# Weight preparation moved from VectorE to GpSimd, and new orders before and after the loop of a decoder layer

## What is computed

```python
x = layernorm(x + mixer(x))        # Mamba-2: W_in, conv of 4 taps, decay, gate, RMS norm, W_out
x = layernorm(x + xattn(ctx, x))   # 8 heads of 64; keys and values of [norm(ctx), norm(x)]
x = layernorm(x + ffn(x))          # 3 cycles: out += coupling * twist(out)

# mixer, the end
y = y * silu(z)
y = y * rsqrt(mean(y * y) + 1e-5) * norm_w
return y @ W_out.T
# ffn
gf = global_net(mean(x))                       # 3 layers, gelu
for _ in range(3):
    tf = coupling_net(out)                     # 4 layers, gelu
    out = out + (0.1 + r * (0.7 * gf + 0.3 * tf - 0.5) * 2) * twist(out)
```

## Time and profile before

| | us |
|---|---|
| median of 3 runs | 3686.03 (3682.52 to 3687.17) |
| profiled execution: its time | 3687.81 |
| profiled execution: span | 3685.6 |
| TensorE busy | 3613.6 (98%) |
| VectorE busy | 3246.4 (88%) |
| ScalarE busy | 3072.9 (83%) |
| GpSimd busy | 1788.0 (49%) |

### The profile page before, as it was taken

One profiled execution on the slowest core, in us unless ns is written; L12 is line 12 of the kernel. 1 busy time (PEld: TensorE's weight loads), 2 busy tenths in 40 slices (PEclk: granted clock), 3 DMA queues, 4 the chain that ended last, 5 costly groups with the idle time before them and its releaser, 6 DMA issues.

```text
span 3685.6 us, 79670 instructions
## 1 busy us (share of the span) xinstructions
PE 3613.6 (98%) x26752; PEld 3085.0 (84%) x26752; DVE 3246.4 (88%) x7970; ACT 3072.9 (83%) x7559; POOL 1788.0 (49%) x3084
## 2 busy tenths in 40 slices
PE   5999999999999999999999999999999999999997
PEld 4888888888888888888888888888888888888885
DVE  7888988988988989889889889889898898898884
ACT  5788888888888888888888888888888888888884
POOL 4355454454554554554544545545545545445442
PEclk8999999999999999999999999999999999999998
DMA  3212212112122122122121121221221221211210
GB/s 100 59 37 67 59 42 67 52 49 67 39 63 64 37 67 64 37 67 58 43 67 53 48 67 39 63 65 37 67 64 37 67 60 42 67 55 46 67 34 21
DMA packets 312358, 203.28 MB, mean 55 GB/s; under 512 B 55056, under 2 KB 310928, under 8 KB 311952
## 3 DMA queue, kind: packets, MB, share of 16 engines
q1 hardware_dynamic: 311952, 198.20, 18.7%
HBM read 180.17 MB, written 17.96 MB: 54 GB/s over the span
## 4 chain that ended last, share of the span: by engine, by line
PE 93%; DVE 3%; ACT 1%; issue 1%; SPq 1%; DMA 1%; POOL 1%; POOLq 0%; DVEq 0%; ACTq 0%
PE psum L263 35%; PE psum L455 10%; PE psum L471 9%; PE psum L443 8%; PE psum L350 6%; PE psum L482 6%; PE psum L518 5%; PE psum L338 5%; PE psum L524 2%; PE psum L533 2%; PE psum L322 1%; PE psum L495 1%; PE psum L383 1%; PE psum L361 1%; PE psum L545 1%
## 5 line engine op out<-in xcount | busy, mean ns | idle before, releaser
L1015 ACT ACTIVATE prob<-psum,nmax 128x376 f32<-128x376 f32 x1024 | 588.7, 582 | 36.0 <-DVE nmax L1741 35.0
L2471 POOL TENSOR_TENSOR Lm<-Lm,G 128x384 f32<-128x384 f32 x512 | 497.3, 1011 | 81.8 <-DVE out_sb L1869 68.8
L1741 DVE TENSOR_REDUCE nmax<-psum 128x2 f32<-128x752 f32 x512 | 472.8, 934 | 44.2 <-PE psum L443 39.4
L455 PE MATMUL psum<-ident,prob 128*128 128x128 f32 (+1 forms) x3072 | 486.4, 278 | 3.1 <-DVE probT L1764 1.7
L455 PEld LDWEIGHTS psum<-ident,prob 128*128 128x128 f32 (+1 forms) x3072 | 354.8, 141 | 87.0 <-issue 46.5
L1493 DVE SCALAR_TENSOR_TENSOR u<-psum,par,u 128x255 f32<-128x255 f32 (+5 forms) x960 | 408.2, 467 | 12.0 <-ACT u L914 1.5
L2458 POOL TENSOR_SCALAR_AFFINE_SELECT Lm<-Lm 128x256 f32<-128x256 f32 x512 | 193.0, 416 | 375.7 <-DMA Lm<-cum_row 375.5
L2526 POOL TENSOR_TENSOR h_a<-h_a,cpl 128x512 f32<-128x512 f32 x64 | 83.0, 1297 | 594.0 <-DVE h_pre L1852 594.0
L471 PE MATMUL psum<-probT,V 128*64 128x256 f32 (+1 forms) x3072 | 360.5, 383 | 0.4 <-ACT probT L1025 0.4
L263 PE MATMUL psum<-x_hi,w_in_hi 128*128 128x256 f32 (+1 forms) x1152 | 344.8, 299 | 13.0 <-DVE w_in_lo L1897 7.6
L263 PE MATMUL psum<-x_hi,w_in_lo 128*128 128x256 f32 (+1 forms) x1152 | 325.4, 282 | 0.0
(11 more groups left out here) (227 smaller groups left out, 11668.6 us busy)
## 6 DMA issues: line engine op xcount, KB each, us to landing
Lm<-cum_row SPq DMA_DIRECT2D x64, 1024.0 KB, 5.2
Lm<-cum_row SPq DMA_DIRECT2D x64, 512.0 KB, 6.6
invT<-inv_row SPq DMA_DIRECT2D x256, 128.0 KB, 3.0
xT_sb<-in_xT SPq DMA_DIRECT2D x64, 256.0 KB, 2.7
x_sb<-in_x SPq DMA_DIRECT2D x64, 256.0 KB, 5.8
result<-out_sb SPq DMA_DIRECT2D x64, 256.0 KB, 2.4
inv_row<-inv_t SPq DMA_DIRECT2D x512, 1.0 KB
ctx_sb<-in_ctx SPq DMA_DIRECT2D x64, 120.0 KB, 6.4
```

The costliest lines, as they stand in the source:

```text
L455: t = tr(banks[b][0:m, j * P:(j + 1) * P], prob[:, r, j0:j0 + m], ident[:, :])
L1015: act(prob[:, r, :], b[:, 0:NK], ACT.Exp, bias=nmax[:, n:n + 1], accum_out=psum_row[:, n:n + 1]).then_inc(a_exp, 1)
L1741: e.tensor_reduce(nmax[:, 2 * n:2 * n + 2], psum[:, b:b + 2, 0:NK], AX.X, ALU.max, negate=True).then_inc(d_max, 1)
L2471: t = tt(Lm[:, h, :], Lm[:, h, :], G[:, :], ALU.mult)
```

## The change

- `w_out_sb`'s scaling and the two subtractions for wkv_lo leave VectorE's `weights` and go, with the same shapes, to GpSimd's `weights`, which becomes `weights(s, n)`. GpSimd runs its old part first (n = 2), then w_out (n = 0), then wkv (n = 1), all ahead of `masked(0, 0)`. They count on a new semaphore, `set_wp`, which `out_proj` (1) and `q_pair`, `k_tile`, `v_tile` (2, beside `set_w` 4) wait for.
- What is left of VectorE's preparation, `weights(0, 3)`, goes from ahead of `cum_dt(0)` to behind `x_dt(0, 1)` and ahead of `gate_silu(0, 0)`. The silu and rounding of B and C and the sums come ahead of most conv taps.
- ScalarE's start has `weights(0, 3)` (wq and wkv high halves) behind `softplus(0)` and `conv(0, 1)`.
- SP has `spread_cum(1)` right behind `load_xT(1)`, and `load_x(1)` behind `load_xT(2)`.
- The end part of all five programs has a new order. The loops are as before, and TensorE's start too.

```diff
 # TensorE
             def out_proj(s):
-                pe.wait_ge(set_w, 4)
+                pe.wait_ge(set_wp, 1)
             def q_pair(s, j):            # k_tile and v_tile alike
-                pe.wait_ge(set_w, 5)
+                pe.wait_ge(set_w, 4)
+                pe.wait_ge(set_wp, 2)
...
             v_tile(last, 2)
             layer(last - 1, 0, 1)
-            turn(last, 6)
-            glob(last - 1, 1)
+            glob(last - 1, 0)
             turn(last, 7)
             layer(last - 1, 0, 2)
+            glob(last - 1, 1)
+            scores(last, 3, 1)
+            turn(last, 8)
             glob(last - 1, 2)
-            turn(last, 8)
-            scores(last, 3, 1)
+            layer(last - 1, 0, 3)
             turn(last, 9)
+            turn(last, 10)
             twisted(last - 1)
-            layer(last - 1, 0, 3)
-            turn(last, 10)
+            turn(last, 11)
             values(last, 0)
-            turn(last, 11)
             layer(last - 1, 1, 1)
             turn(last, 12)
             turn(last, 13)
             layer(last - 1, 1, 2)
             turn(last, 14)
+            layer(last - 1, 1, 3)
             turn(last, 15)
-            layer(last - 1, 1, 3)
+            layer(last - 1, 2, 1)
             values(last, 1)
-            layer(last - 1, 2, 1)
+            layer(last - 1, 2, 2)
+            layer(last - 1, 2, 3)
             w_o(last, 0)
             w_o(last, 1)
-            layer(last - 1, 2, 2)
-            layer(last - 1, 2, 3)
             x2_turn(last)
-            glob(last, 0)
             layer(last, 0, 0)
             layer(last, 0, 1)
+            glob(last, 0)
+            layer(last, 0, 2)
             glob(last, 1)
-            layer(last, 0, 2)
             glob(last, 2)
             layer(last, 0, 3)
             twisted(last)
 # ScalarE, start
+            weights(0, 0)
             x_high(0)
-            weights(0, 0)
             weights(0, 1)
             bcdt(0)
             weights(0, 2)
             conv(0, 0)
-            weights(0, 3)
+            bcdt_th(0)
             softplus(0)
             conv(0, 1)
-            bcdt_th(0)
+            weights(0, 3)
             conv_th(0, 0)
 # VectorE
-                elif n == 3:
-                    ve.wait_ge(w_rest_in, 16 * 13)
-                    for k in range(CT):
-                        t = ts(w_out_sb[:, k, :], w_out_sb[:, k, :], prm("norm_w", k), None, ALU.mult)
-                    t.then_inc(set_w, 1)
...
-                    for k in range(KT):
-                        t = tt(wkv_lo[:, k, :], wkv_raw[:, k, :], wkv_hi[:, k, :].bitcast(F32), ALU.subtract)
-                    t.then_inc(set_w, 1)
...
             bcdt_tap(0, 0)
-            bcdt_tap(0, 1)
             weights(0, 2)
             dt_add(0)
             softplus(0)
-            conv_tap(0, 1, 0)
+            bcdt_tap(0, 1)
             bcdt_tap(0, 2)
-            conv_tap(0, 1, 1)
-            conv_tap(0, 0, 0)
-            conv_tap(0, 1, 2)
-            weights(0, 3)
-            weights(0, 4)
+            bc_silu(0)
+            bc_high(0)
             cum_dt(0)
             cum_da(0)
             cum_scan(0)
...
             x_dt(0, 0)
             x_dt(0, 1)
+            context_stats(0)
+            weights(0, 3)
             gate_silu(0, 0)
 # GpSimd
-            def weights(s):
+            def weights(s, n):
 
                 po.wait_ge(w_rest_in, 16 * 13)
+                if n == 1:
+                    po.wait_ge(set_hi, 4)
+                    for k in range(KT):
+                        t = tt(wkv_lo[:, k, :], wkv_raw[:, k, :], wkv_hi[:, k, :].bitcast(F32), ALU.subtract)
+                    t.then_inc(set_wp, 1)
+                    return
+                if n == 0:
+                    po.wait_ge(par_in_ok, 16)
+                    for k in range(CT):
+                        t = ts(w_out_sb[:, k, :], w_out_sb[:, k, :], prm("norm_w", k), None, ALU.mult)
+                    t.then_inc(set_wp, 1)
+                    return
...
-            weights(0)
+            weights(0, 2)
+            weights(0, 0)
+            weights(0, 1)
             masked(0, 0)
 # SP
             spread_cum(0)
             load_xT(1)
+            spread_cum(1)
+            load_ctx(1)
+            load_xT(2)
             load_x(1)
-            load_ctx(1)
-            spread_cum(1)
-            load_xT(2)
```

More of the change, by code:

```diff
@@ L697, in _ @@
             turn(last - 2, 4)
-            turn(last - 2, 5)
             mean_square(last - 1)
@@ L701, in _ @@
             layer(last - 3, 0, 0)
-            turn(last - 2, 6)
+            turn(last - 2, 5)
             v_tile(last - 2, 2)
@@ L705, in _ @@
             layer(last - 3, 0, 1)
-            turn(last - 2, 7)
-            turn(last - 2, 8)
+            turn(last - 2, 6)
             glob(last - 3, 0)
@@ L711, in _ @@
             scores(last - 2, 3, 1)
+            turn(last - 2, 7)
+            turn(last - 2, 8)
             glob(last - 3, 2)
@@ L752, in _ @@
             y_pair(last, 1)
+            q_pair(last - 1, 1)
+            turn(last - 1, 2)
             y_pair(last, 2)
+            y_pair(last, 3)
             scores(last - 1, 2, 0)
+            v_tile(last - 1, 1)
+            k_tile(last - 1, 3)
             scores(last - 1, 2, 1)
-            y_pair(last, 3)
-            turn(last - 1, 2)
-            k_tile(last - 1, 3)
-            v_tile(last - 1, 1)
+            turn(last - 1, 3)
             x2_turn(last - 2)
-            turn(last - 1, 3)
+            turn(last - 1, 4)
             scores(last - 1, 3, 0)
-            turn(last - 1, 4)
             turn(last - 1, 5)
@@ L804, in _ @@
             scores(last, 1, 0)
+            layer(last - 2, 2, 3)
             turn(last, 1)
@@ L808, in _ @@
             q_pair(last, 1)
-            layer(last - 2, 2, 3)
+            scores(last, 1, 1)
             turn(last, 2)
-            scores(last, 1, 1)
             scores(last, 2, 0)
+            k_tile(last, 3)
             v_tile(last, 1)
-            k_tile(last, 3)
+            scores(last, 2, 1)
             x2_turn(last - 1)
-            scores(last, 2, 1)
             turn(last, 3)
             turn(last, 4)
-            glob(last - 1, 0)
             scores(last, 3, 0)
             turn(last, 5)
+            turn(last, 6)
             layer(last - 1, 0, 0)
@@ L1242, in _ @@
             layer(last - 4, 2, 2)
+            decay(last - 1, 0)
+            values_out(last - 3, 1)
             exp(last - 2, 0)
-            values_out(last - 3, 1)
+            layer(last - 4, 2, 3)
             exp(last - 2, 1)
-            layer(last - 4, 2, 3)
-            decay(last - 1, 0)
+            v_out(last - 2, 0)
             decay(last - 1, 1)
-            v_out(last - 2, 0)
             decay(last - 1, 2)
             cb_out(last - 1)
-            exp(last - 2, 2)
             decay(last - 1, 3)
@@ L1294, in _ @@
             glob(last - 3, 2)
+            turn_out(last - 2, 7)
             exp(last - 2, 13)
@@ L1297, in _ @@
             layer(last - 3, 0, 3)
+            exp(last - 2, 14)
             turn_out(last - 2, 9)
-            exp(last - 2, 14)
             x1_out(last - 1)
@@ L1313, in _ @@
             turn_out(last - 2, 11)
+            layer(last - 3, 2, 0)
             k_out(last - 1, 2)
-            layer(last - 3, 2, 0)
             turn_out(last - 2, 13)
@@ L1388, in _ @@
             turn_out(last - 1, 15)
-            layer(last - 2, 2, 2)
             exp(last, 0)
@@ L1392, in _ @@
             values_out(last - 1, 1)
-            exp(last, 2)
+            layer(last - 2, 2, 2)
             v_out(last, 0)
             turn_out(last, 1)
+            layer(last - 2, 2, 3)
+            exp(last, 2)
             exp(last, 3)
@@ L1400, in _ @@
             exp(last, 6)
+            k_out(last, 3)
             exp(last, 7)
+            exp(last, 8)
             v_out(last, 1)
-            layer(last - 2, 2, 3)
-            exp(last, 8)
-            k_out(last, 3)
+            exp(last, 9)
             x2_out(last - 1)
-            exp(last, 9)
             turn_out(last, 3)
@@ L1410, in _ @@
             exp(last, 11)
+            turn_out(last, 5)
             layer(last - 1, 0, 0)
-            glob(last - 1, 0)
-            turn_out(last, 5)
             keep_a(last - 1)
@@ L1416, in _ @@
             layer(last - 1, 0, 1)
-            glob(last - 1, 1)
+            glob(last - 1, 0)
             turn_out(last, 7)
             layer(last - 1, 0, 2)
+            glob(last - 1, 1)
             exp(last, 12)
             glob(last - 1, 2)
+            layer(last - 1, 0, 3)
+            turn_out(last, 9)
             exp(last, 13)
             exp(last, 14)
-            turn_out(last, 9)
-            layer(last - 1, 0, 3)
             keep_b(last - 1)
@@ L1433, in _ @@
             layer(last - 1, 1, 2)
-            turn_out(last, 15)
             layer(last - 1, 1, 3)
             layer(last - 1, 2, 0)
+            turn_out(last, 15)
+            layer(last - 1, 2, 1)
```

(6 more changed lines are left out.)

476 lines of the change are left out of this document (238 added, 238 removed).

## The result

The changed kernel takes 3693.74 us (median of 22 runs, 3690.14 to 3698.75), the kernel before, timed with it, 3687.52 (22 runs, 3681.56 to 3692.5). The ratio is 1.0018, 95% interval 1.0011 to 1.0024: slower by 6.2 us. The forecast of 3687.0 was too low, and the range ended 0.24 us short.

The account below looks back on a forecast made before the run. TensorE was taken as busy throughout the middle, with idle time only at both ends. Start −4.5 and end +5.5 gave +1.0 on the profiled execution, 3688.8; the median, 1.8 lower, was forecast at 3687.0 us, range 3680.5 to 3693.5.

Parts of the forecast that it names:

- Step (1): Start, VectorE: without the moved weight work the scan ends near 17.4, ten microseconds earlier; the broadcast lands at 26.1.
- (2): Start, GpSimd: moved scalings (3.6 us) and subtractions (5.0) stand ahead of `masked(0)`, which starts at 31.1 instead of 36.20.
- Step (3): Start, VectorE: second `x_dt(0)` ends near 30.6, or 35.6 if GpSimd's subtractions hold VectorE twice; before 40.22.
- step (4): Start, VectorE: six leftover weight instructions, 2.3 us, fall beside `times_g(0)`; 6 more if each waits for GpSimd.
- Step (5): Start's sum: `times_g(0)` ends near 42, not 46.92; steps behind unchanged, lower clock +0.5 to +1.5; gain 4.5 us.
- rival B: Start: GpSimd's long instructions hold VectorE's silus, then the leftovers; gain 1 or none, about 3692 us; chance 0.20.
- step (6): End, TensorE: `values(last,1)` behind `layer(last-1,2,1)` leaves a gap empty, so `w_o(last,0)` starts 4.0 us later.
- step (7): End, ScalarE: `twisted(last-1)` moved behind `layer(last-1,0,3)` and two turns delays h1 of the third cycle; +0.8 us.
- Step (8): Last sequence: `glob(last)` leaves a wait and stands ahead of `layer(last,0,3)`; +0.7 us, between 0.3 and 1.2.
- A: The end does not lose: −4.5 to −6 at the start, little at the end, 3681.5 us; chance 0.20.
- C: Both ends gain, −7 at the start and −1 at the end: 3678 us; chance 0.08.
- D: The new order causes a stall in the busy stretch: +8, 3694 us; chance 0.05.

Follow-up runs that it names:

- e8: e1 with the low half of wkv made by VectorE again, ahead of the first `x_silu`: 3679.00 us, ratio to the kernel before 0.9972 to 0.9989.
- e7: The change with 25 throwaway matmuls that fit TensorE's wait ahead of `layer(last-1,2,1)`, order unchanged: 3689.77 us, ratio to the kernel before 1.0001 to 1.0019.
- e10: e1 with the change's order of `glob(last)` on TensorE and ScalarE alone: 3685.49 us, ratio to the kernel before 0.9985 to 1.0003.
- e15: The change with old places for values, inverses' round trip, `glob(last)`, GpSimd's `att(last)` and VectorE's x2 norm: 3686.52 us, ratio to before 0.9999.
- e3: The change with `values(last,1)` back ahead of `layer(last-1,2,1)` and `w_o(last)` ahead of `layer(last-1,2,2)`: 3694.85 us, ratio to the kernel before 1.0008 to 1.0025.
- e1: The change's start with the five old endings of the kernel before: 3683.59 us, ratio to the kernel before 0.9979 to 0.9997.
- e6: e1 with throwaway matmuls in TensorE's waits of the last sequence: 3674.06 us, ratio to the kernel before 0.9959 to 0.9981.
- e11: e8's start with e6's throwaway matmuls in the last sequence, old endings: 3673.52 us, ratio to the kernel before 0.9948 to 0.9973.
- e12: e11 with throwaway matmuls in TensorE's waits of the first sequence too: 3685.10 us, ratio to the kernel before 0.9983 to 1.0001.
- e2: The start of the kernel before with the change's five new endings: 3698.05 us, ratio to the kernel before 1.0016 to 1.0039.

## Why the prediction was wrong

**The start, right in the number, in part by luck.** Step (1) and (2): scalings 0.91 (0.90 taken), subtractions 2.5, `masked(0)` at 31.52 (31.1). Step (3) went the other of its two ways: `x_dt(0,1)` ended at 35.98, its held case (35.6). Of the 5.4 above the free case (30.6) the two silus' hold is 3.9; the rest is VectorE's wait for ScalarE, 2.03 where 0.6 was taken. In step (4) the leftovers took 2.2 and were not held; it was GpSimd that waited, three of its `times_g` taking 4.06 beside VectorE's 1.21 of `wq_lo`, and three later ones 2.92. By the Trainium skill (SBUF — State Buffer, Who interferes with whom) a VectorE instruction with two SBUF inputs takes part in the lock with GpSimd; 5.25 us for two `x_silu` beside 5.09 on GpSimd agrees, and so does GpSimd's 5.60 in e8.

Step (5) has `out_proj(0)` at 48.6, measured 48.94, a gain of 4.2 (4.5). But its way there was another: it had `times_g(0)` end near 42, and it ended at 44.43, only 2.5 earlier than before. "The steps behind are the same" did not hold either: before, they began with a wait for `load_xT(1)` behind `in_z(0)`, and this wait is gone. `times_g` was 2.4 us later than forecast, and the steps behind it took 4.5 in place of 6.2; the two nearly cancel. What the gain follows is the start of `in_z(0)`, 4.25 earlier, and thus VectorE's chain to `x_dt(0)`. So the first half of rival B, the held silus, stands on the way that counts. Its second half did not come, and so `gate_silu(0,0)` started at 39.03, where B had it end at 44.6.

**Wrong, step (6), the size of the end.** It forecast 3 us of empty wait (3.08), `w_o(last)` later by 4.0, with step (7) 4.8. Measured from `w_o(last-1)`: 7.72. The parts: h1 later by 0.74, step (7)'s 0.8; the new order at the full clock 4.09, step (6)'s 4.0 (from `layer(last-1,2,1)` to `w_o(last)` it takes 5.30 in e7, 1.21 before); and 2.89 for the clock, which e7 gives back. This last term was not in the sum: it took `layer(last-1,2,1)` and the values at 1.13 and 2.82, their durations from the earlier trace rows, where no long wait stood ahead of them. The prediction allowed for the lower clock level at the start (0.5 to 1.5) and forgot it at the end, where it opened a gap itself. The mechanism was right, a term was missing.

**Step (8)** was 0.7; e10 measures 0.89. **Step (7)**: the 0.74 are there one cycle earlier already (the start of `layer(last-1,1,1)` in e15, 0.66 later than before).

**Missed altogether:** the inverses' round trip (VectorE's transposition, SP's `spread_inv`) and GpSimd's `factors` ahead of the norm. In the change they cost nothing, since the late values cover the one and the late `w_o` the other; so the sum did not need them. But it said nothing of them, and the attempt to mend the values' place alone (e3, on the median no gain) ran into them.

**The middle,** taken at 0 between 0 and 2. From the repeated part to `out_proj(last)` the seven kernels with old endings (before, e1, e6, e8, e10, e11, e12) take 335.56 to 336.45 us, mean 336.1, the ten with new ones 336.34 to 337.57, mean 336.8; and from there to `w_o(last-1)` 34.2 against 34.5. That is 1.0 us of loss; which of the moves makes it, no run shows. The repeated part itself spreads from 3026.99 to 3031.51 over the profiles with no regard to the ends (means 3029.3 with the old endings, 3029.0 with the new), so the 2.9 that the first pair of profiles shows there is spread and no effect.

**The sum:** −4.2 at the start, +1.0, +8.75 at the end, in all +5.6, where +6.2 was measured. The forecast sum was +1.0. Besides, the median of three runs it was set against lay 1.5 us below that of all 22, which made the forecast lower still.

**Rivals.** A (the end does not lose) and C are out, by e2. B's first half is there and costs: 4.2 is the gain with the held silus in it, and e8, without them and with less in GpSimd's queue, has 3.3 more. Its second half is not there, nor its start without a gain. D was no part of it: over the busy stretch TensorE's idle time went from 4.4 to 6.8 us.

## What to carry to other kernels

When an edit opens a wait on TensorE, price the work behind it at the lower clock level as well: here a gap of 3.1 us cost 2.9 more in the 7 us behind it. In a tail where TensorE mostly waits, matmuls that nobody reads can be the cheapest edit (7.5 us here), if they need nothing that comes late, a bank included. And an order written for five engines is tied together: a move that was harmless in the new order becomes the next thing late when another is undone, so undo them together or read the queue behind each before you count a gain. Last, a part of a sum that comes out right can have gone another way; look which wait ended last before you trust it.
